# A chunked state-space layer on one core: y opened by the state product, gated by VectorE; last normalisation split between ScalarE and GpSimd

## The reference, cut to what matters

```
x = x + layernorm(attn(layernorm(x)))          # a state-space layer, 32 heads of 8, state 64, rank 2
x = x + layernorm(ffn(layernorm(x)))

attn: z, x_raw, B, C, dt, lam, theta = x @ W_in          # B and C are normalised and rotated
      y = y_intra(C, B, x) + y_inter(C, state)           # within a chunk, and from the state before it
      y = rms(y * silu(z));  return y @ W_out
ffn:  r = sigmoid(xr @ W_r);  k = square(relu(xk @ W_k));  return r * (k @ W_v)
```

## Time and profile before

| | |
|---|---|
| runs | 249.55, 249.6, 250.18 us, median 249.6 |
| the profiled execution | 250.03 us, its span 248.2 us |
| busy of the span: PE, PEld | 218.3 us (88%), 159.9 us (64%) |
| DVE, ACT, POOL | 208.9 us (84%), 188.6 us (76%), 160.3 us (65%) |
| granted TensorE clock, mean | 0.978 |

### The profile page before, as it was taken

How to read it: one execution, slowest core, us unless ns; L and a number is a source line. 1 busy time by engine, 2 the same in 40 slices (tenths; PEclk the granted TensorE clock), 3 DMA queues, 4 the chain that set the end, 5 groups by cost and what they waited for, 6 DMA issues and landing times. The chain is left out here.

```text
span 248.2 us, 6592 instructions
## 1 busy us (share of the span) xinstructions
PE 218.3 (88%) x1962; PEld 159.9 (64%) x1962; DVE 208.9 (84%) x646; ACT 188.6 (76%) x728; POOL 160.3 (65%) x275
## 2 busy tenths in 40 slices
PE   0895998679999999999999999999999999999930
PEld 0893443456767666768777876877687768657920
DVE  1789999987779988986999899989989997956880
ACT  2366776669988699877988798789779977989661
POOL 7433134757798698776769686968686866563530
PEclk9999799999999999999999999999999999999985
DMA  5980000000000000000000001000100110010123
GB/s 121 228 275 4 3 0 0 1 3 1 3 3 3 0 3 1 3 0 5 1 3 0 3 3 45 3 0 1 46 3 1 23 23 0 3 44 4 42 50 87
DMA packets 10199, 6.45 MB, mean 26 GB/s; under 512 B 864, under 2 KB 9856, under 8 KB 10160
## 3 DMA queue, kind: packets, MB, share of 16 engines
q1 hardware_dynamic: 10016, 5.77, 9.6%
q0 software_dynamic: 144, 0.21, 0.4%
HBM read 3.88 MB, written 2.10 MB: 24 GB/s over the span
## 5 line engine op out<-in xcount | busy, mean ns | idle before, releaser
L978 PE MATMUL bank<-x,sg 64*64 64x256 f32 x256 | 35.0, 391 | 0.6 <-DVE sg L1393 0.6
L1386 DVE TENSOR_TENSOR x<-bank,wx 128x512 f32<-128x512 f32 x32 | 21.9, 685 | 15.5 <-ACT bank L672 12.5
L672 ACT ACTIVATE bank<-bank,rsn 128x512 f32<-128x512 f32 x32 | 21.1, 658 | 17.0 <-PE bank L879 17.0
L978 PE MATMUL bank<-xg,sg 64*64 64x256 f32 x256 | 33.0, 376 | 0.0
L966 PE MATMUL pair<-x,turned_bc 64*64 64x256 f32 x224 | 29.6, 376 | 0.0
L544 POOL TENSOR_TENSOR y<-ysum,zs 128x256 f32<-128x256 f32 x32 | 23.8, 742 | 5.5 <-DVE ysum L1409 5.5
L455 POOL TENSOR_TENSOR rb<-mse,halfn 128x2 f32<-128x2 f32 x32 | 23.7, 741 | 2.5
L452 POOL TENSOR_TENSOR mse<-msb,eps_all 128x2 f32<-128x2 f32 x32 | 8.1, 253 | 25.5 <-ACT junk L663 25.4
L1071 PE MATMUL bank<-wo_sb,yt 128*128 128x128 f32 x128 | 22.7, 300 | 0.0
L1386 DVE TENSOR_TENSOR xg<-bank,wx 128x512 f32<-128x512 f32 x32 | 21.8, 680 | 0.0
L427 POOL TENSOR_TENSOR x_lo<-xnT_all,x_hi 128x128 fp32r<-128x128 f32 x32 | 14.7, 460 | 10.4 <-ACT x_hi L587 10.4
(11 more groups left out here) (195 smaller groups left out, 750.2 us busy)
## 6 DMA issues: line engine op xcount, KB each, us to landing
x_all<-x SPq DMA_DIRECT2D x16, 128.0 KB, 4.1
out<-o_all SPq DMA_DIRECT2D x14, 128.0 KB, 2.6
cm<-consts SPq DMA_DIRECT2D x1, 640.0 KB, 6.3
w_sb<-w_in SPq DMA_DIRECT2D x1, 480.0 KB, 4.0
out<-o_all SPq DMA_DIRECT2D x4, 64.0 KB, 2.1
cm<-consts POOLq DMA_DIRECT2D x1, 128.0 KB, 4.0
wo_sb<-w_out SPq DMA_DIRECT2D x1, 128.0 KB, 4.7
bcb_sb<-bc_bias SPq DMA_DIRECT2D x1, 96.0 KB, 4.6
```

The source lines that it names most:

```text
L672: nc.scalar.activation(x_ps[:], x_ps[:], ACT.Silu, scale=rsn[:, par:par + 1]).then_inc(S["x_silu"], 1)
L978: mm = nc.tensor.matmul(y_ps[half(h)], sg[half(h), a, r], rx(x, r)[half(h)], start=start, stop=stop)
L1386: vec.tensor_tensor((x1, xg)[a][:, par].rearrange("p (a e) -> p a e", e=P), x_ps[:].rearrange("p (a e) -> p a e", e=P), wx[:, par, a].unsq ...
```

## The change

Three things are changed together. First, the state product of tile n + 1 is issued within `mix(n)`, between own 0 and own 1, and opens y's bank of tile n + 1 (start flag set there; the other products add to it). y has two banks, 6 and the first half of 2, by the tile's parity; B and C's transposes move to the first half of bank 5, and `turn(n)` waits for the mask of tile n - 1 where it waited for a copy of ScalarE. `mix` issues the next state earlier: earlier 0, next state 0, earlier 1, next state 1, own 0, state product of the next tile, own 1. Second, VectorE multiplies y by the gate straight from y's bank; ScalarE's copy, the sum on VectorE and the product on GpSimd are gone. Third, for the FFN units 0 to 2 (chunks 0 to 2, done while chunks 4 to 6 run) VectorE's `last_residual` is gone: ScalarE computes f * rstd + bias (`scaled_f`) where `outputs` stood, and GpSimd adds x, two tiles in the step with q = 3 and two in the next one with q = 1.

```diff
+POOL_UNITS = 3
...
-        t_ps, inter_ps = bank[2][:, 0:DI], bank[2][:, DI:]
+        t_ps = bank[5][:, 0:DI]
...
-        y_ps, ffn_ps = bank[6][:, 0:DI], bank[7]
+        y_ps, ffn_ps = (bank[6][:, 0:DI], bank[2][:, 0:DI]), bank[7]
...
+                    return j + 1, hi(rounds[j][2]), rounds[j][3]
+            return 0, 0, -1
...
+        def wait_added(eng, u):
+
+            if u < POOL_UNITS:
+                wait_past(eng, C["scaled_f"], hi(u))
+            else:
+                eng.wait_ge(C["res"], hi(u) - hi(POOL_UNITS - 1))
...
+            def add_residual(u, part):
+                for i in range(lo(u), hi(u))[part]:
+                    pool.wait_ge(C["scaled_f"], i + 1)
+                    pool.wait_ge(C["x1"], i + 1)
+                    nc.gpsimd.tensor_tensor(o_all[:, i], o_all[:, i], x_all[:, i], ALU.add).then_inc(C["outv"], 1)
...
+                if q == 3 and 0 <= c - 4 < POOL_UNITS:
+                    add_residual(c - 4, slice(0, 2))
+                if q == 1 and 0 <= c - 5 < POOL_UNITS:
+                    add_residual(c - 5, slice(2, 4))
...
-                gated(NT - 1, NQ - 1, 1)
...
-            def gated(n, q, par):
-                pool.wait_ge(S["ysum_ready"], n + 1)
-                if not isinstance(n, int) or n >= 2:
-                    pool.wait_ge(S["yt_ps"], n - 1)
-                    pool.wait_ge(S["ysq_done"], n - 1)
-                nc.gpsimd.tensor_tensor(y[:, par], ysum[:, par], zs[:, q], ALU.mult).then_inc(S["y_ready"], 1)
...
-            def state_part(n, par):
-                act.wait_ge(S["inter_ps"], n + 1)
-                if not isinstance(n, int) or n >= 2:
-                    act.wait_ge(S["ysum_ready"], n - 1)
-                nc.scalar.activation(zt[:, par], inter_ps, ACT.Copy).then_inc(S["zt_sb"], 1)
...
-                if within(n):
-                    state_part(n, q % 2)
...
+            def scaled_f(u):
+                act.wait_ge(C["norm_bias"], round3(u) + 1)
+                act.wait_ge(C["x1"], hi(u))
+                for i in range(lo(u), hi(u)):
+                    k = column3(i)
+                    nc.scalar.activation(o_all[:, i], ff[:, slot(i)], ACT.Identity, scale=frs[:, k:k + 1],
+                                         bias=fnb[:, k:k + 1]).then_inc(C["scaled_f"], 1)
...
                 if q == 2 and valid(c - 4):
-                    outputs(c - 4)
+                    (scaled_f if c - 4 < POOL_UNITS else outputs)(c - 4)
...
             def turn(n, q):
                 pe.wait_ge(S["bc_turned"], n + 1)
                 pe.wait_ge(S["t_sb"], n)
-                pe.wait_ge(S["zt_sb"], max(n - 1, 0))
+                pe.wait_ge(S["sg_ready"], n)
...
+            def from_state(par, state, stop):
                 for h in range(2):
-                    mm = nc.tensor.matmul(to[half(h)], bt[half(1 - h), par, h, half(h)], state[half(1 - h)], start=True,
-                                          stop=True)
+                    mm = nc.tensor.matmul(y_ps[par][half(h)], bt[half(1 - h), par, h, half(h)], state[half(1 - h)],
+                                          start=True, stop=stop)
...
+            def state_part(n):
+
+                if n >= NQ:
+                    pe.wait_ge(S["st_ready"], n - NQ + 1)
+                else:
+                    pe.wait_ge(S["st_zero"], 2)
+                    pe.wait_ge(t_turn[1], 3)
+                pe.wait_ge(S["t_sb"], n + 1)
+                wait_past(pe, S["y_ready"], n - 1)
+                from_state(n % 2, st[:, n % NQ], False).then_inc(S["inter_ps"], 1)
...
             def mix(n, q, par):
 
                 def earlier_tokens(r):
-                    within_chunk(0, r, x1[:, par], start=(r == 0), stop=False)
+                    within_chunk(par, 0, r, x1[:, par], start=False, stop=False)
 
                 def own_token(r):
-                    return within_chunk(1, r, xg[:, par], start=False, stop=(r == R - 1))
+                    return within_chunk(par, 1, r, xg[:, par], start=False, stop=(r == R - 1))
 
                 def next_state(r):
                     if carries(n):
@@ -993,26 +1010,19 @@
                         if r == R - 1:
                             mm.then_inc(S["p_ps"], 1)
 
-                def state_product():
-                    if n >= NQ:
-                        pe.wait_ge(S["st_ready"], n - NQ + 1)
-                    else:
-                        pe.wait_ge(S["st_zero"], 2)
-                        pe.wait_ge(t_turn[1], 3)
-                    pe.wait_ge(S["t_sb"], min(n + 2, NT))
-                    from_state(inter_ps, par, st[:, q]).then_inc(S["inter_ps"], 1)
-
+                pe.wait_ge(S["inter_ps"], n + 1)
                 pe.wait_ge(S["x1_ready"], n + 1)
-                pe.wait_ge(S["ysum_ready"], n)
+                pe.wait_ge(S["y_ready"], n)
                 pe.wait_ge(S["sg_ready"], n + 1)
+                pe.wait_ge(S["p_added"], min(n, NT - NQ))
                 earlier_tokens(0)
-                state_product()
+                next_state(0)
                 earlier_tokens(1)
-                pe.wait_ge(S["p_added"], min(n, NT - NQ))
-                next_state(0)
+                next_state(1)
                 pe.wait_ge(S["xg_ready"], n + 1)
                 own_token(0)
-                next_state(1)
+                if n + 1 < NT:
+                    state_part(n + 1)
                 own_token(1).then_inc(S["y_ps"], 1)
...
-                    pe.wait_ge(S["zt_sb"], NT)
+                    pe.wait_ge(S["y_ready"], NT)
...
-                    pe.wait_ge(S["ysum_ready"], NT)
+                    pe.wait_ge(S["y_ready"], NT)
...
                     (mix_general if general else mix)(n, q, par)
+                elif not general:
+                    state_part(0)
...
-            def summed_y(n, par, general):
+            def gated_y(n, q, par, general):
                 dve.wait_ge(S["y_ps"], n + 1)
-                if not general:
-                    dve.wait_ge(S["zt_sb"], n + 1)
+                dve.wait_ge(S["zec_ready"], n + 1)
                 if not isinstance(n, int) or n >= 2:
-                    dve.wait_ge(S["y_ready"], n - 1)
-                vec.tensor_tensor(ysum[:, par], y_ps, yk[:] if general else zt[:, par],
-                                  ALU.add).then_inc(S["ysum_ready"], 1)
+                    dve.wait_ge(S["yt_ps"], n - 1)
+                    dve.wait_ge(S["ysq_done"], n - 1)
...
+                vec.tensor_tensor(y[:, par], yk[:] if general else y_ps[par], zs[:, q], ALU.mult).then_inc(S["y_ready"], 1)
...
+                wait_added(dve, n3)
+                if n3 >= POOL_UNITS:
+                    dve.wait_ge(C["outv"], hi(n3))
...
-                wait_past(dve, C["res"], hi(ahead(u)))
+                wait_added(dve, ahead(u))
...
-                if q == 1 and valid(c - 4):
+                if q == 1 and valid(c - 4) and c - 4 >= POOL_UNITS:
                     last_residual(c - 4)
```

More of the change, by code:

```diff
@@ L494, in rstd @@
                 wait_past(pool, C["normed"], n2)
-                wait_past(pool, C["res"], n3)
+                wait_added(pool, n3)
                 t = slice(rounds[k][0], rounds[k][1])
@@ L1054, in mix_general @@
                 for r in range(R):
-                    mm = within_chunk(1, r, xg[:, par], start=(r == 0), stop=(r == R - 1))
+                    mm = within_chunk(par, 1, r, xg[:, par], start=(r == 0), stop=(r == R - 1))
                 mm.then_inc(S["y_ps"], 1)
```

35 lines of the change are left out of this document (15 added, 20 removed).

## The result

| | before | after |
|---|---|---|
| median of 6 runs each | 249.57 us (249.22 to 250.18) | 248.59 us (248.46 to 248.84) |
| ratio | | 0.9944, 95% interval 0.9926 to 0.9963 |
| profiled execution, span | 250.03, 248.2 | 248.84, 246.3 |

By the medians the change gains 1.0 us, a quarter of the 4.0 forecast; by the ratio, which is estimated from the runs and is not the quotient of the medians (0.9961), it gains 1.4 us, 0.9 to 1.8. Its interval leaves out 1, so the change is faster, and 248.59 lies in the range of 243.0 to 248.8, near its slow end. Of the two profiled executions 1.9 us come off the span and 0.7 us go back outside it (1.8 before, 2.5 after; 2.0 to 2.5 in the six runs of the changed kernel). No view shows what lies outside the span.

What follows compares the result with a forecast made beforehand. TensorE was taken to bind in tiles 11 to 27, VectorE 1 to 2 us behind. Gains 0.1 + 0.75 + 1.95 + 0.8 + 0.4 = 4.0 us took 250.03 to 246.0, median 245.6; range 243.0 to 248.8 (own range 243.8 to 247.8).

Steps and rivals of the forecast that it cites:

- Tiles 0 to 11: Early stage, walked through the engine queues: 0.1 us faster by tile 14, with 2 us of doubt either way.
- (b): B/C transposes now wait for the current tile's mask: 0.67 us later in tile 1, 1.15 with tile 0's loss.
- Chunk 3: Chunk 3's term: the scores' ended waits give 1.1 us, of which the transposes' mask wait lets 0.75 be kept.
- Tiles 20 to 28: Part of the term for chunks 4 to 6, forecast at 0.65 us gained per chunk, 1.95 in all.
- (a): Next state's second half ahead of own-token products ends 17 scores' waits in steps 11 to 27: 4.5 us.
- (d): ScalarE loses 32 copies; dearer normalisation costs 0.37 us per four in chunks 4 to 6; net 0.1 later before the projection.
- (e): Chunks 4 to 6: VectorE loses twelve 0.46 us ops, worth nothing; GpSimd gets twelve adds of 0.61, nothing due behind them.
- Tiles 28 to 31: Chunk 7's term: three ended scores' waits left, worth 0.8 us with the transposes' mask wait counted.
- Tail: End of the kernel: last two y leave VectorE, not GpSimd; the next chain moves by only 0.4 us, the gain taken.
- (f): VectorE's residuals, slowed by busy GpSimd (about 1.1 of 2.18 us), take 0.3 less per chunk, bounds 0 and 0.7.
- B: Rival, chunks 4 to 6: dearer ScalarE normalisation and o copy delay x's gate and y's copy, no gain there; 247.6 us; 0.13.
- C: Rival, tiles 0 to 9: transposes pay the mask wait in full, 4.1 us lost, 3.5 gained later; 250.2 us; chance 0.08.

Runs made afterwards that it cites:

- fill_behind: Changed kernel with VectorE's two blocks of one-off early work (token weights, angle operations) moved from ahead of a step to behind its mask: 247.51 us, ratio 0.9905.
- late_first: Changed kernel with the old last normalisation, one-off work behind the masks, and B/C transposes behind the projection of B and C for tiles 1 to 11 only: 243.95 us.
- fill_pool0: Changed kernel with VectorE's one-off work behind the masks and the last normalisation as before, transposes ahead of the projection of B and C throughout: 244.74 us, ratio 0.9794.
- pool0: Changed kernel with the last normalisation as before for all chunks (VectorE joins x), the y part kept: 246.42 us, ratio 0.9874.
- late_pool0: Changed kernel with the last normalisation as before and the B/C transposes behind the projection of B and C: 246.03 us, ratio 0.9846.
- all3_later: Changed kernel with the old last normalisation, one-off work behind the masks, and B/C transposes behind both their projection and y's transposes: 246.03 us, ratio 0.9852.
- order_only: Kernel before with only the second half of the next state's product issued ahead of the own-token products: 249.87 us, ratio 0.9991.
- mask_wait: Kernel before with one wait added: a tile's B/C transposes also wait for the mask of the tile ahead: 253.38 us, ratio 1.0156.
- state_last: Kernel before with the current tile's state product issued behind both halves of the next state's product, y still joined from two banks: 254.08 us, ratio 1.0177.
- weights_late: Changed kernel with VectorE's token weights for the second half of the tiles moved from ahead of tile 0's mask to behind step 0: 250.15 us, ratio 1.0017.
- no_add: Changed kernel without GpSimd's additions of x (12 output tiles lack x), ScalarE's scale-and-bias normalisation kept: 247.58 us, ratio 0.9898.
- turn_late: Changed kernel with a tile's B/C transposes issued behind, not ahead of, the projection of B and C of the tile after it: 247.23 us, ratio 0.9892.
- norm_only: Kernel before with only the new last normalisation of three chunks (ScalarE scales and biases, GpSimd adds x), y untouched: 251.18 us, ratio 1.005.

## Why the prediction was wrong

By the terms of the sum, with the measured column of the changed kernel beside each:

- **Tiles 0 to 11: -0.1 forecast, +1.07 measured** (+0.78 at tile 14, the place that the forecast names). The step that failed is (b) with the walk that followed it. I left out that tiles 0 and 1 have five one-off operations of VectorE ahead of their masks, which before had to be done only by the time of the products. fill_behind shows that this is 1.25 us, the fall of the clock that goes with it included: with that work out of the way the balance is -0.18, nearly the number forecast. That the two numbers are so near is in part luck, since late_first has -1.30 there: in fill_behind the transposes still wait 1.8 us for masks up to 58 us, and other gains make up for it. (fill_pool0 against pool0 gives 1.72; pool0 itself has 0.49 more there than the changed kernel with the same early program.)
- **Chunk 3: -0.75, measured -0.85**, and tiles 16 to 20 -0.65, measured -0.73. Right.
- **Tiles 20 to 28: -1.3, measured -0.97.** (a) was worth more than I let it keep: pool0 has -1.15 and -1.16 a chunk, the full 1.1 of the waits counted. What I took off for (b) and (d) is not lost in the kernel without the new normalisation. But (e) was costed at nothing with "nothing is queued behind them that is due": GpSimd's own factors are, 0.4 us later, and VectorE's two-operand work beside them is held, 0.39 and 0.43 us a chunk. The rule of the Trainium skill (SBUF — State Buffer, SBUF: two separate sides) stood in my text as speaking against these additions, and the sum left it out because no row had one; a bound should have gone in. The 0.36 a chunk of (d) is right in size and was put at the wrong place: in steps 19, 23 and 27 the projection follows the products after 0.05 us and does not wait for y's copy, and it is y's transposes that wait for the squares of o.
- **Tiles 28 to 31: -0.8, measured +0.03.** A miscount: (a) has 17 waits, 16 of them in chunks 3 to 6 as I had already spent them, so one was left and not three. pool0 shows it: -0.39, the size of one wait of the earlier trace rows. In the changed kernel ScalarE's 0.36 takes it back.
- **Tail: -0.4, measured -0.34**, of which the 0.3 that unchanged kernels show cannot be told from chance. pool0 and late_first, -0.71, and late_pool0, -0.66, show a gain of this size beyond that; all3_later has -1.44, which I have not looked into.
- **Outside the span: nothing forecast, +0.7 in the profiled pair.** The runs of order_only, mask_wait and state_last have 1.8 to 1.9, as before; those of the other kernels 1.8 to 2.6. I have not found what it is, and it stays open.
- **(f)** is right by an error that did not matter. Four residuals at the 0.62 for two are 1.24, so 0.9 of the 2.18 is GpSimd's doing and not 1.1; the 0.3 a chunk that I used is what came: 556 ns before, 479 after, four of them.

Of the 2.8 us by which the profiled execution missed the forecast, 1.2 are the early tiles, 0.8 tiles 28 to 31, 0.7 lie outside the span and 0.3 are in tiles 20 to 28, where (a)'s larger gain hid most of what (e) costs; the other terms make up the rest.

Mechanism (a) was right in effect and wrong in cause. The scores do stop waiting. What does it is not that the next state goes ahead of the own tokens (order_only: nothing) but that the state product leaves its place ahead of the next state in the crossed quarters (state_last: 1.99 us, though y pays), and the second bank for y with the gate on VectorE makes that affordable; this last part is argued, since no run has one of them alone.

Of the rivals, B had a mechanism of the late chunks (ScalarE's normalisation ahead of o) and 247.6 us, C the mechanism of the early loss and a price of 4.1 us. mask_wait has 4.10 for the wait alone, but that agreement is chance: its execution has the halved clock in it, and 3.56 of it is there at the transposes of tile 2, where C spread it over tiles 0 to 9. Neither happened alone. The result is a part of B and a part of C together, and I had given the forecast 0.67 as if they excluded one another.

## What to carry to other kernels

When a wait is added on the full engine, look for what stands ahead of the awaited instruction in its queue in the first few rounds: one-off work that was harmless behind the old deadline is in the way of the new one, and moving it behind the awaited instruction cost nothing here, whereas moving it to the next step (weights_late) only moved the loss. Products on quarters of the array run in lanes: in order_only and state_last an instruction moved in program order moved in time only when it changed its place within its own lane. Work taken from a nearly full VectorE and given to a less busy GpSimd was no gain here, where VectorE has two-operand work beside it; try such parts one at a time, since here one part (-3.2 us) hid that the other cost 2.2.

## What the runs showed of the hardware that I had not expected

The clock. After TensorE idled for the mask of tile 0 its granted clock fell to 0.50 (the 1.2 GHz level) in the changed kernel, and in no_add, with the same program and the same waits up to there, it did not:

```profile
50.00:52.00 2.00, 2.00 (x21) 1.29 (x24) 1.87 (x5) 1.29 (x8) 0.89 (x3) 0.50 0.00 0
```

```profile
50.00:52.00 2.00, 2.00 (x34) 1.33 (x34) 1.56 (x4) 1.54 (x10) 0.78 (x3) 1.00 0.00 0
```

(windows of 2 us, the first of the changed kernel, the second of no_add: busy time of TensorE, its weight loads, VectorE, ScalarE, GpSimd, then the granted clock). I expected the dip to be some 1.6 us of the early loss. In this pair none of it shows: the balance at tile 12 is +1.07 with the dip and +1.21 without. In no_add the products end sooner, and the next transposes wait longer for the same mask:

```profile
49.34 0.41 PE L945 MATMUL pair<-cm,turned_bc 128*128 128x128 f32 x2 [1.45 <-DVE sg L1400]
55.71 0.41 PE L945 MATMUL pair<-cm,turned_bc 128*128 128x128 f32 x2 [2.46 <-DVE sg L1400]
```

From 50.1 to 54.8 us VectorE of the changed kernel has no gap in which it waits, so a slower TensorE is hidden behind it.

That is not so everywhere. turn_late and late_pool0 have the same steps up to tile 16, and in both the transposes of tile 2 wait 1.96 us for the mask. In turn_late (first of each pair) the clock stays, in late_pool0 it falls right behind:

```profile
54.92 0.41 PE L949 MATMUL pair<-cm,turned_bc 128*128 128x128 f32 x2 [1.96 <-DVE sg L1404]
59.31 0.38 PE L949 MATMUL pair<-cm,turned_bc 128*128 128x128 f32 x2
56.00:58.00 2.00, 2.00 (x37) 1.60 (x29) 1.75 (x5) 1.97 (x12) 1.39 (x4) 1.00 0.03 8
```

```profile
54.40 0.41 PE L949 MATMUL pair<-cm,turned_bc 128*128 128x128 f32 x2 [1.96 <-DVE sg L1404]
60.42 0.38 PE L949 MATMUL pair<-cm,turned_bc 128*128 128x128 f32 x2
56.00:58.00 2.00, 2.00 (x25) 1.19 (x17) 0.83 (x3) 1.97 (x10) 1.45 (x4) 0.50 0.00 0
```

The next transposes come 6.02 us later instead of 4.39, VectorE is busy 0.83 of 2 us instead of 1.75, and 1.37 us of it are still there at tile 12. The six executions of late_pool0 fit: the three with a mean granted clock of 0.971 have spans of 244.2 and 244.3 us, the others (0.975 to 0.982) 242.6 to 243.3. So the halved clock was hidden in the one pair, where VectorE set the pace, and cost 1.6 us in the other, where TensorE did.

How long TensorE had waited does not tell whether the clock falls: it fell after 1.45 us in the changed kernel and 1.46 in pool0, and stayed after 1.45 and 2.46 in no_add and after 1.96 in turn_late. fill_behind, whose TensorE never idles over 0.92 us from 46 to 58 us, kept 1.00 throughout; one execution of each is no proof that it always does. The offset in the first column of the table goes with the clock too. Five executions had a granted clock of 0.50 from 28 to 32 us, where the kernel before has 0.78 and then 1.00 (no_add, norm_only, order_only, turn_late, late_first), and their offsets are +0.27 to +0.89. Of the others only state_last, with +0.27, is above zero.
